# A graph block in one kernel: two weight remainders computed on GpSimd, the first masks on VectorE, twenty more warming products, two hl steps moved up

## What is computed

```
h   = relu(layernorm(x))                              # 6250 nodes x 256
out1 = segment_sum(edge_attr, dst)                    # 100000 edges x 96, sorted by dst
out2 = segment_max(edge_attr, dst), 0 where no edge
out3 = out1 / max(count, 1)
h'  = relu(concat[h, out1, out2, out3, u[0]] @ W1 + b1) @ W2 + b2     # W1 608 x 1024, W2 1024 x 256
y   = x + h' + h
```

## Time and profile before

| | before |
|---|---|
| median of 3 runs | 566.95 us |
| the profiled execution, and its span | 566.98 us, 565.2 us |
| TensorE busy | 488.0 us, 86% |
| VectorE busy | 469.5 us, 83% |
| ScalarE busy | 347.7 us, 62% |
| GpSimd busy | 250.4 us, 44% |
| chain that ended last | TensorE 58%, VectorE 18%, DMA 7%, ScalarE 7%, issue 6%, GpSimd 3% |

### The profile page before, as it was taken

One profiled execution on the slowest core, in us unless ns is written; L12 is line 12 of the kernel. 1 busy time (PEld: TensorE's weight loads), 2 busy tenths in 40 slices (PEclk: granted clock), 3 DMA queues, 4 the chain that ended last, 5 costly groups with the idle time before them and its releaser, 6 DMA issues.

```text
span 565.2 us, 8843 instructions
## 1 busy us (share of the span) xinstructions
PE 488.0 (86%) x3042; PEld 449.5 (80%) x3042; DVE 469.5 (83%) x904; ACT 347.7 (62%) x944; POOL 250.4 (44%) x253
## 2 busy tenths in 40 slices
PE   0027977989999998977999999999999999999991
PEld 0026867889999998977888888888888888888991
DVE  4979979898999999898999998989989889792220
ACT  1934584767778685675848757568576795743330
POOL 2454634444362727375175472771743705102021
PEclk9998997989999999998999999999999999999997
DMA  2954333535351625545146442461451515001010
GB/s 99 278 159 133 124 130 96 178 105 181 99 209 50 222 80 183 203 159 186 58 161 212 137 146 107 166 214 24 178 198 50 156 63 169 23 1 37 1 39 18
DMA packets 18837, 71.13 MB, mean 126 GB/s; under 512 B 4571, under 2 KB 5755, under 8 KB 18776
## 3 DMA queue, kind: packets, MB, share of 16 engines
q0 software_dynamic: 15408, 65.72, 35.1%
q1 hardware_dynamic: 3378, 4.79, 2.9%
HBM read 64.09 MB, written 6.85 MB: 126 GB/s over the span
## 4 chain that ended last, share of the span: by engine, by line
PE 58%; DVE 18%; DMA 7%; ACT 7%; issue 6%; POOL 3%; DVEq 0%; POOLq 0%; ACTq 0%
PE l1ps L579 23%; PE l1ps L583 11%; PE yps L599 11%; DVE work L809 10%; DMA work<-in_edge_attr,idx 6%; PE yps L603 6%; PE tps L560 3%; PE l1ps L588 3%; ACT work L423 2%; ACT cat L394 2%; POOL work L324 2%; DVE work L798 1%; POOL out_y L338 1%; DVE cat L809 1%; DVE inl L898 1%
## 5 line engine op out<-in xcount | busy, mean ns | idle before, releaser
L324 POOL DMA_INDIRECT work<-in_edge_attr,idx x98 | 118.8, 1213 | 197.4 <-DVE cat L809 148.8
L809 DVE TENSOR_TENSOR work<-work 128x768 f32<-128x768 f32 (+14 forms) x174 | 151.4, 902 | 1.0
L432 ACT ACTIVATE hff<-l1ps,b1e 128x512 f32<-128x512 f32 (+2 forms) x120 | 72.6, 605 | 111.1 <-PE l1ps L588 105.3
L423 ACT ACTIVATE work<-work,mk 128x96 f32<-128x96 f32 x427 | 120.3, 367 | 21.8 <-DMA work<-in_edge_attr,idx 21.7
L579 PE MATMUL l1ps<-inh,w1h 128*128 128x512 f32 (+2 forms) x480 | 118.3, 370 | 1.7 <-ACT hh L434 1.0
L579 PE MATMUL l1ps<-inh,w1l 128*128 128x512 f32 (+2 forms) x480 | 113.7, 360 | 0.0
L583 PE MATMUL l1ps<-inl,w1h 128*128 128x512 f32 (+2 forms) x480 | 112.4, 357 | 0.0
L894 DVE TENSOR_TENSOR hl<-hff,hh 128x512 fp32r<-128x512 f32 (+2 forms) x120 | 71.3, 594 | 39.1 <-ACT hh L434 33.5
L338 POOL DMA_INDIRECT out_y<-xr,oidx x49 | 68.5, 1398 | 76.9 <-DVE xr L925 62.9
L599 PE MATMUL yps<-w2h,hh 128*128 128x256 f32 x392 | 98.6, 282 | 0.0
L599 PE MATMUL yps<-w2l,hh 128*128 128x256 f32 x392 | 98.0, 280 | 0.0
(11 more groups left out here) (138 smaller groups left out, 462.3 us busy)
## 6 DMA issues: line engine op xcount, KB each, us to landing
work<-in_L_gnn_W SPq DMA_DIRECT2D x2, 1024.0 KB, 6.3
work<-in_edge_attr,idx POOLq DMA_INDIRECT x98, 5.3
xr<-in_L_gnn_W SPq DMA_DIRECT2D x1, 1024.0 KB, 11.0
xr<-in_x,nid POOLq DMA_INDIRECT x49, 4.1
out_y<-xr,oidx POOLq DMA_INDIRECT x49, 3.2
work<-in_dst SPq DMA_DIRECT2D x1, 415.0 KB
dstp<-in_dst SPq DMA_DIRECT2D x1, 415.0 KB
hff<-in_L_gnn_W SPq DMA_DIRECT2D x3, 128.0 KB, 7.5
```

The costliest lines, as they stand in the source:

```text
L324: pool.indirect_dma_start(out=ell[g % 2][:, at:at + kk * F], out_offset=None, in_=edge, in_offset=bass.IndirectOffsetOnAxis(ap=idx[:, a + ...
L423: last = act.activation(es[g % 2][:, at * F:(at + 1) * F], ell[g % 2][:, src:src + F], ACT.Copy, scale=mk[:, a + j, e:e + 1])
L432: act.activation(hf[C % 2][:, 0:cols], l1ps[C % 2][:, 0:cols], ACT.Relu, bias=b1e[:, m:m + 1])
L809: return V.tensor_tensor(out=slots(buf, n, per, 0, size // 2) if out_ is None else out_, in0=slots(buf, n, per, 0, size // 2), in1=slots(b ...
```

## The change

The low part of `w1r` and the low part of W2 are subtracted on GpSimd instead of VectorE: the first directly behind `w1l` and ahead of the first gather, the second behind the gathers of batch 0 and ahead of the wait for the flag. ScalarE copies `w1r` ahead of the second half of `w1h`. The masks of group 0 are one VectorE instruction over both tiles instead of eight on ScalarE and one on VectorE. The number of warming products goes from 26 to 46. `lo(7)` and `lo(8)` stand ahead of `in_low(1, 0)` and behind `residual(1)` instead of inside the loop.

```diff
-    WARM = 26
+    WARM = 46
...
+            pool.wait_ge(w_hi, 1)
+            pool.wait_ge(w_pool, 2)
+            pool.tensor_tensor(out=w1r[KR:2 * KR, :], in0=raw1r[KR:2 * KR, :], in1=w1r[KR:2 * KR, :], op=ALU.subtract).then_inc(w_pool, 1)
+            pool.wait_ge(w_pool, 3)
             pool.wait_ge(idx_ready, 1)
             gather_x(0, [0])
...
             gather_x(0, list(range(1, width(0))))
+            pool.wait_ge(w_hi, 3)
+            pool.tensor_tensor(out=w2l[:, :, :], in0=raw2, in1=w2h[:, :, :], op=ALU.subtract).then_inc(w_pool, 1)
             pool.wait_ge(flag_ready, 1)
...
+            act.wait_ge(w1r_in, 48)
+            act.activation(w1r[:, :], raw1r[0:3 * KR, :], ACT.Copy).then_inc(w_hi, 1)
             act.wait_ge(w1b_in, 16)
             act.activation(w1h[:, 2:4, :], raw1[1], ACT.Copy).then_inc(w_hi, 1)
-            act.wait_ge(w1r_in, 48)
-            act.activation(w1r[:, :], raw1r[0:3 * KR, :], ACT.Copy).then_inc(w_hi, 1)
...
-            mask(0, 0, 2)
             root(0)
...
-                dve.wait_ge(masked, g + 1)
                 if g == 0:
-                    at = (k1 + k2 + k1) * F
                     dve.wait_ge(ell_in[0], ell_count(0))
-                    V.tensor_tensor(out=s[:, k2 * F:2 * k2 * F]..., in0=e[:, at:at + k2 * F]..., in1=mk[:, a + 1, 0:k2, None]..., op=ALU.mult)
+                    V.tensor_tensor(out=s[:, 0:n * k2 * F]..., in0=e[:, 0:n * (k1 + k2) * F]...[:, :, k1:k1 + k2, :], in1=mk[:, a:a + n, 0:k2, None]..., op=ALU.mult)
...
-            V.tensor_tensor(out=w1r[KR:2 * KR, :], in0=raw1r[KR:2 * KR, :], in1=w1r[KR:2 * KR, :], op=ALU.subtract).then_inc(w_lo, 1)
...
-            V.tensor_tensor(out=w2l[:, :, :], in0=raw2, in1=w2h[:, :, :], op=ALU.subtract).then_inc(w_lo, 1)
...
             lo(5)
             lo(6)
+            lo(7)
             in_low(1, 0)
             in_low(1, 1)
             moments(2)
             residual(1)
+            lo(8)
             scales(2)
...
-                    if s * HC + m - 1 < NCH:
+                    if HC < s * HC + m - 1 < NCH:
                         lo(s * HC + m - 1)
```

More of the change, by code:

```diff
@@ L367, in _ @@
                     if s == 0:
-                        pool.wait_ge(w_lo, 3)
+                        pool.wait_ge(w_pool, 4)
                     gather_x(s + 2, list(range(width(s + 2))))
@@ L411, in mask @@
                 a, n, k1, k2, _, _ = groups[g]
-                if g == 0:
-                    act.wait_ge(mask_ready, 1)
                 if g == 1 and piece == 0:
                     act.wait_ge(bias_ps, 1)
-                if g == 2:
-                    act.wait_ge(mask_ready, 2)
+                if g <= 2:
+                    act.wait_ge(mask_ready, g)
                 if piece == 0:
@@ L423, in mask @@
                     last = act.activation(es[g % 2][:, at * F:(at + 1) * F], ell[g % 2][:, src:src + F], ACT.Copy, scale=mk[:, a + j, e:e + 1])
-                if piece == pieces - 1 or g == 0:
+                if piece == pieces - 1:
                     last.then_inc(masked, 1)
@@ L586, in layer1 @@
                 if C == 0:
-                    pe.wait_ge(w_lo, 2)
+                    pe.wait_ge(w_pool, 3)
                 pe.matmul(ps, w1r[:, ks(m)], inr[b % 2][:, 0:cols], start=False, stop=True).then_inc(l1_done, 1)
@@ L618, in _ @@
                     pe.wait_ge(w_hi, 3)
-                    pe.wait_ge(w_lo, 3)
+                    pe.wait_ge(w_pool, 4)
                 if C == HC:
@@ L786, in tree_head @@
                 e, s = ell[g % 2], es[g % 2]
-                dve.wait_ge(masked, g + 1)
                 if g == 0:
-                    at = (k1 + k2 + k1) * F
                     dve.wait_ge(ell_in[0], ell_count(0))
-                    V.tensor_tensor(out=s[:, k2 * F:2 * k2 * F].rearrange("p (e f) -> p e f", f=F), in0=e[:, at:at + k2 * F].rearrange("p (e f) -> p e f", f=F),
-                                    in1=mk[:, a + 1, 0:k2, None].broadcast_to([P, k2, F]), op=ALU.mult).then_inc(dve_step, 1)
+                    V.tensor_tensor(out=s[:, 0:n * k2 * F].rearrange("p (n e f) -> p n e f", n=n, f=F),
+                                    in0=e[:, 0:n * (k1 + k2) * F].rearrange("p (n e f) -> p n e f", n=n, f=F)[:, :, k1:k1 + k2, :],
+                                    in1=mk[:, a:a + n, 0:k2, None].broadcast_to([P, n, k2, F]), op=ALU.mult).then_inc(dve_step, 1)
                     dve.wait_ge(dve_step, next(step))
+                else:
+                    dve.wait_ge(masked, g)
                 for lo in range(0, k1, k2):
@@ L939, in _ @@
             tree_tail(0)
-            dve.wait_ge(w_hi, 1)
+            dve.wait_ge(w_hi, 2)
             V.tensor_tensor(out=w1l[:, 2:4, :], in0=raw1[1], in1=w1h[:, 2:4, :], op=ALU.subtract).then_inc(w_lo, 1)
@@ L943, in _ @@
             in_low(0, 1)
-            dve.wait_ge(w_hi, 2)
-            V.tensor_tensor(out=w1r[KR:2 * KR, :], in0=raw1r[KR:2 * KR, :], in1=w1r[KR:2 * KR, :], op=ALU.subtract).then_inc(w_lo, 1)
             dve.wait_ge(mb_step, 2)
@@ L949, in _ @@
             V.tensor_tensor(out=b1e[:, :], in0=yps[0][:, 0:HC], in1=b1c[:, :], op=ALU.add).then_inc(bias_set, 1)
-            dve.wait_ge(w_hi, 3)
-            V.tensor_tensor(out=w2l[:, :, :], in0=raw2, in1=w2h[:, :, :], op=ALU.subtract).then_inc(w_lo, 1)
             overlap(late).then_inc(mask_ready, 1)
```

## The result

| | before | after |
|---|---|---|
| median of 5 runs | 566.94 us | 571.73 us |
| profiled execution, span | 566.98 us, 565.2 us | 571.73 us, 569.9 us |
| ratio after / before, 95% interval | | 1.0077 [1.0061, 1.0092] |

The changed kernel is slower by 0.8%. The ratio is not the quotient of the two medians (1.0084), which lies inside its interval. Measured again later it was 571.69 us (6 runs) against 567.28 us (17 runs), ratio 1.0079 [1.0062, 1.0096].

What follows compares the result with a forecast made beforehand. A chain of waits alternating through TensorE, VectorE and gathers, almost VectorE alone from 30 to 93 us, was taken as the bound. +3.05 and +0.8 us on 565.2, plus 1.8 outside the span, gave 570.8 us; range 565.0 to 571.8.

Steps and rivals of the forecast that it cites:

- both blocks: VectorE waits for both GpSimd subtractions, w1r and w2l; the forecast case, between 569.5 and 572 us, 40 in 100.
- The block on w1r: Start-up: VectorE's `key` waits for GpSimd's subtraction of w1r, late by 2.0 us (bounds 0 and 2.3).
- The block on w2l: Ahead of the flag: VectorE's `mk` waits until GpSimd's subtraction of w2l ends at 42.54, +3.8 us.
- The masks: Group 0's masks on VectorE: first tree addition at 46.5 instead of 41.05, +5.45 us; without any VectorE waiting 40.7, -0.33.
- The rival that VectorE never waits: VectorE is not held up by GpSimd's subtractions anywhere; 565.1 us, 25 in 100.
- the rival that GpSimd is held up: VectorE's mask and L798 stop GpSimd's w2l for 3.5 us, gathers of group 1 6.7 us later; 569.3 us, 15 in 100.
- Warming: Twenty more products fill TensorE's gap before the transposes; `inl` no longer waits for ScalarE's copy, -0.38 us.
- The tree of group 1: VectorE's tree begins at 64.4 instead of 61.35, +3.05 us, containing the start-up steps ahead of it.
- what is late next: Ahead of group 1's tree: ScalarE's masks become late, so of 3.45 us off VectorE about 1.4 are lost.
- lo(7) and lo(8): Ahead of group 2's tree: lo(7) gains nothing; lo(8) makes VectorE wait 1.05 us, +0.8 us (bounds 0.4 and 1.5).
- The sum: Whole kernel: 3.05 + 0.8 = +3.85 us on the 565.2 us span, plus 1.8 outside it, 570.8 us.
- my two cases of 2.4 and 4.3: Start-up on TensorE: twenty more products take about 2.4 us once the clock is up, 4.3 at 0.216 us each.

## Why the prediction was right

The forecast was 570.8 us, and the likeliest case, both blocks, is what happened. The measured 571.73 us is 0.9 us more and lies only 0.07 us inside the upper end of the range (571.8): the mechanism was right, and that the range held is in part luck.

**The block on w1r.** Predicted +2.0 us on `key`; measured 2.15. It was another instruction than I had named: the first of the two that write `key` (26.46 us in before) and not the second (26.80). GpSimd's subtraction started at 26.56 (predicted 26.54). The kernel with only this move is 0.3% slower.

**The block on w2l.** Predicted +3.8 us on `mk`; measured 3.69. Both instructions came half a microsecond later than I had them (`mk` 39.27 for 38.77), which comes from the start-up's 0.16 us, the extra 0.15 us on `key`, and `di` and the small rows beside the gathers.

**The masks.** The load of the flag took 1.55 us (predicted 1.42) and L802 began at 47.04 (predicted 46.5): +5.99, or +5.83 without the later start-up, where I had +5.45. Without the blocks the masks' gain is 0.18 us, where I had 0.33. The rival that VectorE never waits falls with `key` and `mk`; the rival that GpSimd is held up falls with 4.50 us for `w2l`, since `w1l` of the same shape took 4.52.

**Warming.** Mis-sized: 0.38 us was the one wait that I could see. Counted from the first tree level (41.05 us in before, 41.01 with the products) it is 0.62 us at the tree of group 1 in the order of before. Of it 0.47 us is the distance of the two `inl`, 1.07 us against 0.60, and the rest lies ahead of the first. In the changed order the products are worth 2.1 us there and 0.3% of the time (1.0110 against 1.0079, a difference hardly clear of noise). VectorE is no longer the late one there: with its 3.4 us less work ScalarE's masks are what is late, and they stand behind TensorE's first chunk. I had written that TensorE's own speed matters little, which was true of the kernel before only.

**The tree of group 1.** From +5.99 the start came back to +3.19, by 2.80 us; I had 2.40. ScalarE's masks start 0.67 us nearer to the first tree level (warming), they take 1.07 us less from first to last (`b1e`), and the 1.1 us by which VectorE came after them is gone. So the argument on what is late next was right: of 3.4 us off VectorE, VectorE now waits 1.17 us for masks (predicted 1.4).

**lo(7) and lo(8).** lo(8)'s wait was 1.10 us (predicted 1.05). TensorE's wait for hl fell by 4.2 us, and that for the means grew by 5.0 us, as predicted for `lo(7)`. From the tree of group 1 to the end of the tree of group 2 the changed kernel loses 4.06 - 3.19 = 0.87 us (predicted 0.8).

**The sum.** +3.85 predicted at the end of the tree of group 2, +4.06 measured, +3.90 without the later start-up. That it is so near is partly luck: the first tree came 0.4 us later than forecast, and 0.4 us more than forecast was won back behind it. Behind it the assumption that a delay is carried on one to one held only roughly: +5.36 us at the output near 120 us, +4.7 at the end; the repeated run +4.3 and +3.0. Part of this arises near 100 us, in the same DMA as above: from the end of the last gather (102.08 us) to ScalarE's mask (106.35) it is 4.27 us against 3.19 in before, and 3.66 in the repeated run. Gains of under 1 us did not get past this place; the loss of 4 us did.

**Readings that were off.** None of these changes the forecast by more than 0.03 us. `w1r` takes 1.22 us on VectorE, and the 1.25 of the prediction is the distance from its start to the next start. The delay of the first gather without a wait on VectorE's side is 28.64 + 0.30 - 28.36 = 0.58 us and not 0.56. The 26 warming products follow one another at 0.216 us, like the layer-1 products of 55.1 to 55.9 us where the granted clock is 0.50 (0.21 us), and I took this for 1.2 GHz; but the granted clock recorded for 43 to 49 us is 1.00, the level of 2.4 GHz. Which of the two is right there stays open. Twenty more products took 2.7 us more in the order of before (8.43 against 5.70 us), between my two cases of 2.4 and 4.3.

## What to carry to other kernels

GpSimd's pauses are not free if GpSimd reads SBUF: ask what VectorE runs in the same microseconds, and price the move at up to the whole GpSimd instruction on VectorE's side (here 2.15 of 2.34 us, 3.7 of 4.50, and in one kernel all of it), even for a VectorE instruction of 0.2 us. In all these traces such a block is inside the victim's duration and not in its idle time, so compare durations of like instructions with the kernel before; a longer duration with an end 0.1 us behind a GpSimd end is the mark of it. And before pricing work taken off an engine, find what comes second at its next meeting point: here it took 1.2 of 3.4 us.

## What the runs showed that I had not expected

The blocked instruction ends 0.07 to 0.10 us after the recorded end of GpSimd's: `key` 28.97 and 28.90, `mk` 43.14 and 43.04, `t` 40.44 and 40.36, `dg` 28.69 and 28.61. In the trace of before `eloc` ended at 26.08 and `w1l` at 26.01. I had read its 0.21 us as speaking against a block, and it speaks neither way: held until 0.07 us behind `w1l` or not held at all, an instruction of 0.21 us that started at 25.87 ends at 26.08. Where `eloc` started a little sooner it did take longer. VectorE in the kernel with only w2l moved back, whose `w1l` ends at 26.10:

```profile
25.76 0.41 DVE L679 TENSOR_TENSOR eloc<-cnt,lorow 128x50 f32<-128x50 f32 x1
```

The order of the recorded starts doesn't tell who waits. In the kernel with w1r moved back `t` is recorded 0.49 us ahead of `w2l` and is nevertheless the one that waits.

The other direction, too, is longer than I had it: with a mask of 1.76 us on VectorE the first gather of group 1 takes 2.42 us (after, 45.43) in place of 0.94, and ends 0.84 us behind the mask. VectorE's next two-operand addition (47.04) ran beside the rest of this gather in its usual 1.76 us, and the short two-operand instructions beside the gather of 37.54 kept 0.20 us. So it is the gather that waits, near its start, and a running gather did not hold up a VectorE instruction with two SBUF operands. The Trainium skill, page "SBUF — State Buffer", section "Who interferes with whom", infers that `tensor_tensor` leaves the generation of descriptors alone, since this needs the write side. These gathers do wait: each one that met a long `tensor_tensor` with two SBUF operands at its start ended 0.80 to 0.85 us behind it, in all traces up to 62 us. But they also read their row numbers (`idx`, `nid`) from SBUF, and no run here separates this reading from the writing of descriptors.

A GpSimd subtraction on 32 partitions x 1024 took 2.34 us and one on 128 x 2048 4.50 us: half the elements per partition took about half the time, and having only a quarter of the partitions brought nothing on top.
